# A vision tower on one Trainium2 core: LayerNorm rows on ScalarE, four score quarters in one piece, another order

## What is computed

```python
h = tok(x)                       # 3x3 depthwise convolution, then mean of 8x8 blocks: 64 tokens an image
h = h + attn0(layernorm(h))      # one head of 128
h = h + moe(layernorm(h))        # 2 shared and 8 routed experts of 512, the best 2 of 8 for each token
h = h + attn1(layernorm(h))      # 8 heads of 16; 64 keys and 15 compressed keys, a sink; rotary
h = h + mlp(layernorm(h))        # two lower-triangular 128x128 matrices along the channels, GELU

def layernorm(x):
    m, v = mean(x), var(x)       # over the 128 channels
    return (x - m) / sqrt(v + 1e-5)
```

## Time and profile before

| | us |
|---|---|
| median of 3 runs | 1969.28 |
| lowest and highest of them | 1950.70, 1969.51 |
| the profiled execution | 1981.56 |
| its span, first to last instruction | 1979.8 |

### The profile page before, as it was taken

How to read it: one execution, slowest core, us unless ns; L and a number is a source line. 1 busy time by engine, 2 the same in 40 slices (tenths; PEclk the granted TensorE clock), 3 DMA queues, 4 the chain that set the end, 5 groups by cost and what they waited for, 6 DMA issues and landing times.

```text
span 1979.8 us, 42922 instructions
## 1 busy us (share of the span) xinstructions
PE 1588.2 (80%) x14896; PEld 1190.4 (60%) x14896; DVE 1417.9 (72%) x3372; ACT 1002.2 (51%) x2581; POOL 797.3 (40%) x643
## 2 busy tenths in 40 slices
PE   0132878989898988989898989898898989998846
PEld 0021665757666675767576676667676766666623
DVE  3767677878877787888778788778887787642322
ACT  0112546555555646565555547365656555564622
POOL 2335363544526263545436263625444352504020
PEclk9975888998879797998889789879989897979965
DMA  7556564453735544554536455445546364202000
GB/s 295 216 192 230 195 221 181 162 208 145 260 134 193 211 170 163 196 202 155 211 143 227 172 188 220 143 178 201 205 141 231 140 240 156 62 7 62 13 22 6
DMA packets 109125, 331.56 MB, mean 167 GB/s; under 512 B 13662, under 2 KB 87585, under 8 KB 92412
## 3 DMA queue, kind: packets, MB, share of 16 engines
q1 hardware_dynamic: 86416, 300.90, 41.3%
q0 software_dynamic: 8992, 19.42, 2.9%
q10 hardware_dynamic: 13516, 8.50, 1.4%
HBM read 299.48 MB, written 29.29 MB: 166 GB/s over the span
## 4 chain that ended last, share of the span: by engine, by line
PE 43%; DVE 18%; POOL 15%; issue 11%; DMA 6%; ACT 5%; ACTq 2%; SPq 0%; POOLq 0%; DVEq 0%
PE hid_bank L597 10%; PE sec_bank L651 5%; POOL yg L1375 5%; POOL xbuf L1364 4%; DMA xbuf<-in_x 4%; PE hid_bank L582 3%; PE sec_bank L671 3%; PE sec_bank L662 3%; PE hid_bank L581 3%; DVE xbuf L1064 3%; DVE xbuf L1060 3%; POOL rows_d L1353 2%; DVE xc L1269 2%; POOL rs L1336 2%; PE hid_bank L583 2%
## 5 line engine op out<-in xcount | busy, mean ns | idle before, releaser
L1364 POOL TENSOR_TENSOR xbuf<-xbuf 128x512 f32<-128x512 f32 x256 | 343.3, 1341 | 587.3 <-DVE xbuf L1060 578.7
L597 PE MATMUL hid_bank<-w_s,hid 128*128 x1920 | 329.5, 324 | 0.0
L842 ACT ACTIVATE hid<-hid_bank,bias_t 128x128 f32<-128x128 f32 x960 | 272.1, 377 | 83.2 <-PE hid_bank L583 78.9
L597 PEld LDWEIGHTS hid_bank<-w_s,hid 128*128 128x128 f32 x1920 | 278.4, 223 | 18.7
L581 PE MATMUL hid_bank<-xt,w_b 128*128 128x128 bf16 x960 | 221.1, 239 | 57.8 <-ACT ys L852 30.3
L1060 DVE TENSOR_TENSOR xbuf<-xbuf 128x1536 f32<-128x1536 f32 x128 | 224.3, 1752 | 19.8 <-DMA xbuf<-in_x 19.8
L1353 POOL DMA_INDIRECT rows_d<-x2r,spot_i x128 | 159.5, 1246 | 195.8 <-DVE owned L1211 163.4
L582 PE MATMUL hid_bank<-xt,w_b 128*128 128x128 bf16 x960 | 222.2, 240 | 0.4
L583 PE MATMUL hid_bank<-xt,w_b 128*128 128x128 bf16 x960 | 218.4, 236 | 0.0
L1085 DVE SCALAR_TENSOR_TENSOR taps<-pooled_s,tapw,taps 128x256 f32<-128x256 f32 (+1 forms) x416 | 208.6, 501 | 8.3
L1068 DVE TENSOR_TENSOR xbuf<-xbuf 128x1024 bf16<-128x1024 f32 x128 | 173.5, 1355 | 24.2 <-DMA xbuf<-in_x 24.2
(11 more groups left out here) (216 smaller groups left out, 3344.2 us busy)
## 6 DMA issues: line engine op xcount, KB each, us to landing
xbuf<-in_x SPq DMA_DIRECT2D x128, 2048.0 KB
rows_s<-rows_d SPq DMA_DIRECT2D x48, 320.0 KB, 8.1
outs_d<-ys SPq DMA_DIRECT2D x240, 64.0 KB, 1.8
out<-h ACTq DMA_DIRECT2D x16, 256.0 KB
w_s<-in_w ACTq DMA_DIRECT2D x1, 2560.0 KB
hid<-in_w POOLq DMA_DIRECT2D x10, 256.0 KB, 3.4
rows_d<-x2r,spot_i POOLq DMA_INDIRECT x128
yg<-outs_d,spot_i POOLq DMA_INDIRECT x128
```

The lines of the kernel that those rows point to most:

```text
L597: mm = nc.tensor.matmul(hid_bank[n % 2][:, 0:P], hid[:, n % RING, q * P:(q + 1) * P], w_q, start=False, stop=q == FC - 1)
L842: ins = nc.scalar.activation(hid[:, n % RING, cols], hid_bank[n % 2][:, cols], ACT.Gelu, bias=bias_t[:, q, j:j + 1])
L1364: nc.gpsimd.tensor_tensor(v[:, :, 1, :], v[:, :, 1, :], v[:, :, 2 * k + 3, :], ALU.add) \
```

## The change

Three things change. First, `normalise` moves from DVE to ScalarE. DVE makes nb = -mean x inverse root, one instruction of 128x4 (`centre`), and ScalarE gives x times the inverse root plus nb (`Identity` with a scale and a bias per row), four instructions a set. There are four new ScalarE pieces, `norm1` to `norm4`, for x1, x2, x3 and x3.

Second, a `score` piece holds both halves of the heads: two masks, one to each bank, and then the four combinations of two images and two halves. There are four such pieces in place of eight on PE; DVE keeps its eight. The two halves lie in different rows of the array, the two images in different columns.

Third, the lists in `ORDER` are new for all five engines.

```diff
 ORDER = dict(
     pool="""
-        scatter.3' scatter.4' scatter.5' scatter.6' scatter.7' gather.0 gather.1 gather.2 gather.3 gather.4
+        scatter.6' gather.0 scatter.7' gather.1 gather.2 gather.3 gather.4 add.0.0 add.0.1 gather.5 gather.6
...
                 elif kind == "score":
-                    t, half = n // 2, n % 2
-                    bank = sec_bank[half]
+                    t = n
...
-                    if n >= 2:
-                        eng.wait_ge(s3_step, at(s3_step, g, 2 * (n - 2) + 2))
-                    wide, rows = bank[:, 0:HH * (LK + 1)], slice(half * C // 2, (half + 1) * C // 2)
-                    nc.tensor.matmul(wide, place_b[:], limit_b[:, half].rearrange("p h k -> p (h k)"),
-                                     start=True, stop=False)
+                    for half in range(2):
+                        if n >= 1:
+                            eng.wait_ge(s3_step, at(s3_step, g, 2 * (2 * n - 2 + half) + 2))
+                        nc.tensor.matmul(sec_bank[half][:, 0:HH * (LK + 1)], place_b[:],
+                                         limit_b[:, half].rearrange("p h k -> p (h k)"), start=True, stop=False)
                     for im in range(2):
                         tok = (2 * t + im) * L
-                        mm = nc.tensor.matmul(
-                            wide[im * L:(im + 1) * L].rearrange("p (h k) -> p h k", h=HH)[:, :, 0:LK],
-                            q3[rows, tok:tok + L], keys_h[rows, :, 2 * t + im, :],
-                            start=False, stop=True)
-                    mm.then_inc(scored, 1)
+                        for half in range(2):
+                            rows = slice(half * C // 2, (half + 1) * C // 2)
+                            wide = sec_bank[half][im * L:(im + 1) * L, 0:HH * (LK + 1)]
+                            mm = nc.tensor.matmul(wide.rearrange("p (h k) -> p h k", h=HH)[:, :, 0:LK],
+                                                  q3[rows, tok:tok + L], keys_h[rows, :, 2 * t + im, :],
+                                                  start=False, stop=True)
+                            if im == 1:
+                                mm.then_inc(scored, 1)
...
+            def normalise(g, dst, src, nb, rs, centred, ready):
+
+                eng.wait_ge(centred, at(centred, g, 1))
+                for t in range(T):
+                    nc.scalar.activation(dst[:, t, :], src[:, t, :], ACT.Identity, bias=nb[:, t:t + 1],
+                                         scale=rs[:, t:t + 1]).then_inc(ready, 1)
...
-            def normalise(g, dst, src, mv, rs, rstd, ready, read=None, need=0):
+            def centre(g, nb, mv, rs, rstd, centred):
                 eng.wait_ge(rstd, at(rstd, g, 1))
-                if read is not None and after(g, 1):
-                    eng.wait_ge(read, at(read, g - 1, need))
-                for t in range(T):
-                    nc.vector.tensor_scalar(dst[:, t, :], src[:, t, :], mv[:, t, 0:1], rs[:, t:t + 1],
-                                            ALU.subtract, ALU.mult).then_inc(ready, 1)
+                nc.vector.scalar_tensor_tensor(nb[:], mv[:, :, 0], -1.0, rs[:], ALU.mult, ALU.mult).then_inc(centred, 1)
```

92 lines of the change are left out of this document (52 added, 40 removed).

## The result

The kernel after takes 1904.11 us (median of 4 runs, 1898.11 to 1911.73), the kernel before 1969.39 (4 runs, 1950.70 to 1989.49): the ratio is 0.9668, with a 95% interval of 0.9628 to 0.9708. The forecast was 1911. Its profiled execution took 1911.73 us, with a span of 1910.0 and a mean granted clock of 0.93 (0.866 before).

The account below looks back on a forecast made before the run. PE was taken to bound the steady part; -3.8 (scores) -2.5 (head) -1.3 (xc) +0.8 +1.7 +1.2 = -3.9 us an iteration, times 15 = 58, gave 1911 us. Range 1845 to 1978, likeliest case 1885 to 1940.

Parts of the forecast that it names:

- quarters, PE's work: Score pieces on PE: four array quarters run side by side, four pieces replace eight; 3.8 us less an iteration.
- DVE empties the banks: Between score pieces: PE waits for DVE to empty both banks, mostly covered by other work; 0.8 us more an iteration.
- split ahead of score.0, exponentials ahead of att.7: Before the first score piece and att.7: PE waits for ScalarE's key split and exponentials; 1.7 us more an iteration.
- xc: Compressed keys on PE: xc comes before DVE's second rotation, so PE's wait for it goes; 1.3 us less an iteration.
- first lift waits for h: Iteration's first lift on PE: POOL's adds come sooner, the wait for h falls from 2.1 to 0.8 us.
- `out'` waits for taps: Transposes of `out'`, two down pieces later on PE: wait for the last tap goes, 1.2 us less; bound 0.
- LayerNorm longer through ScalarE: norm3 and norm4, on the chain to PE: each set 0.6 us longer through ScalarE, 1.2 us more an iteration.
- The rival of no change: Score stage stays as long as DVE's emptying makes it; only the head gains: 1968, or up to 1950; chance 18%.
- Head: Start of the iteration: PE's waits for h and for the last taps shrink, together 2.5 us less an iteration.
- Keys: Compressed keys and score start: PE's wait for xc goes (-1.3 us), waits for ScalarE's split and exponentials come (+1.7).
- The rival (17%): Clock no longer falls at the scores once PE's xc wait goes: 3.6 us more gain an iteration, 1864 us; 17%.
- The slower rival: SP's queue at the iteration turn: x and rows.0 land late, +3.6 us an iteration, 2023 us; chance 18%.

Follow-up runs that it names:

- e9: Changed kernel with only the new order left: score halves one after the other, LayerNorm on DVE; 1959.89 us, 0.9607 of the kernel before, second chip.
- e4: Changed kernel with the LayerNorm rows back on DVE, so new order and quarters; 1943.64 us, 0.9540 of the kernel before, second chip.
- e1: Changed kernel with the two score halves of a piece one after the other, LayerNorm on ScalarE kept; 1966.29 us, 0.9669 of the kernel before, second chip.
- e3: Kernel before with only the LayerNorm rows moved to ScalarE; 1995.81 us, 1.0144 of the kernel before.
- e10: Changed kernel with `out'` later as in e6 and the LayerNorm rows back on DVE; 1916.32 us, 0.9732 of the kernel before.
- e6: Changed kernel with `out'` two pieces later on PE and one on ScalarE; 1896.83 us, 0.9615 of the kernel before.
- e12: Changed kernel with POOL's list of the kernel before; 1917.67 us, 0.9749 of the kernel before.
- e13: Changed kernel with DVE's second rotation and first inner work put back ahead of xc; 2000.53 us, 1.0157 of the kernel before.
- e5: Kernel before with six extra matmuls on PE in place of its wait for xc; 1967.56 us, 0.9935 of the kernel before.

## Why the prediction was right, step by step

The total was right: 1911 against 1904.11, inside the likeliest case's own range. Its terms were not, and errors of some us each cancel, so that the total came this close is luck. It gave 3.9 us an iteration where the traces have 5.7 (65 us by the medians, over 15 iterations, is 4.4). Each term per iteration:

| step | forecast | measured |
|---|---|---|
| quarters, PE's work | -3.8 | -3.1 (by the pieces), -3.3 (e9 to e4), -4.3 (e1 to after, two chips) |
| the same in time | -3.8 | -1.1 (e9 to e4) |
| DVE empties the banks | +0.8 | 0.4 (4.4 / 12) |
| split ahead of score.0, exponentials ahead of att.7 | +1.7 | 1.3 ((5.4 + 5.2 + 4.6) / 12) |
| xc | -1.3 | -1.3 (15.9 / 12, gone) |
| first lift waits for h | -1.3 | -0.9 (22.4 to 11.1 in 12) |
| `out'` waits for taps | -1.2 | +0.9 (18.8 to 29.3 in 12) |
| LayerNorm longer through ScalarE | +1.2 | +0.4 (e9 to e1), +1.8 (e3), -1.3 (e10 to e6) |
| clock | 0 | PE's work -4.4 (before to e9, two chips), time -2.6 (long stretches, within before) |
| waits behind the scores | 0 | +2.2 (26.6 / 12) |

The rows don't form one sum, since part of the new waits is what the quarters' saved work turned into. In PE's own account the work falls by 8.6, some 3.1 of it by the quarters and the rest with the clock, and the waiting grows by 2.9.

**Scores.** The numbers on PE were near: four quarters in 0.76 us, 1.07 a piece without a wait (1.17 forecast), 3.1 us less work. (Its own figures, 8.3 and 4.7, give 3.6; it took 3.8. The 1.04 that it started from had a small lift in it, and a piece alone took 0.92.) The step that failed is that the work taken away from PE was put down as time, since "PE, not DVE, is the bound". PE was the bound of the iteration, not of this stage: in the new order DVE's list takes 13.8 us there with or without quarters. The rival of no change had named this mechanism with 18%; it holds for the score term, 2.7 us of the 3.8, though not for the kernel.

**Head.** The forecast counted two waits of PE and took both away. The first fell as said (0.9 left, 0.8 forecast). The second had 0 as its bound, with the words that a late tap list moves along; it did more than that. One more tap stands behind the turn of the iteration on DVE now, ends.0.0 (1.28 us) stands ahead of the last tap where it stood behind it, and the two adds, brought forward as forecast, run beside DVE's taps and stretch them by 2.1 us (e12 undoes that). Both waits are ends of one chain on DVE, and e6 and e12 shift the wait from one to the other. A step that names only who waits, and not what DVE has to do in that stretch, can't see this.

**Keys.** Right, both in the wait that went and in the one that came at score.0. But e13 shows that this step can't be priced by the row of before: there PE waits 1.3 us behind seven pieces of other work between `att.4` and the compressed keys, and the new list has spent the filler elsewhere. Undone in the new order the step costs 91 us, not 20.

**Clock.** The rival (17%) gave 3.6 us an iteration from the two levels of the earlier trace rows and named the wait for xc as the cause. The size was about right: the low stretch of the score stage is gone in every iteration, and PE works 4.4 us less from before to e9. (By the kernel before alone it is 2.6 us of time an iteration. The prediction set one of the two shortest of the twelve iterations against the mean, and it put PE's busy time at 95 to 98, where one iteration has 101.3.) The cause isn't borne out: e5 fills the wait and keeps the long low stretch; e13 has a wait four times as long and no long stretch in the scores. The stretch goes with the order of the lists; which of their moves does it was not isolated. In the sum it stood at 0. So more of the gain came by the clock than by the scores.

**LayerNorm.** ScalarE's work rose from 61.7 to 67.0 us, 5.3 (6.2 forecast), DVE's fell by 3.7 and not 5.2. Rows of the kernel after, from a grouping by line and shape over the twelve iterations (busy us, mean ns), and two of the kernel before for the same lines over eleven (L1068 is now L1085, L1364 now L1381):

```profile
L1381 POOL TENSOR_TENSOR xbuf<-xbuf 128x512 f32<-128x512 f32 x192 | 302.9, 1578 | 271.5 <-DVE xbuf L1077 265.1
L1077 DVE TENSOR_TENSOR xbuf<-xbuf 128x1536 f32<-128x1536 f32 x96 | 168.1, 1751 | 13.5 <-DMA xbuf<-in_x 13.1
L1085 DVE TENSOR_TENSOR xbuf<-xbuf 128x1024 bf16<-128x1024 f32 x96 | 155.8, 1623 | 0.0
...
L785 ACT ACTIVATE x<-h,nb,rs 128x128 f32<-128x128 f32 x144 | 59.5, 499 | 4.6 <-DVE nb L1070 4.5
```
```profile
L1364 POOL TENSOR_TENSOR xbuf<-xbuf 128x512 f32<-128x512 f32 x176 | 231.5, 1315 | 367.7 <-DVE xbuf L1060 362.0
...
L1068 DVE TENSOR_TENSOR xbuf<-xbuf 128x1024 bf16<-128x1024 f32 x88 | 119.8, 1362 | 2.9 <-DMA xbuf<-in_x 2.8
```

The activation with two pointers takes 499 ns, 480 forecast. That DVE lost less than counted is the row of L1085: it takes 261 ns longer each, 8 x 0.26 = 2.1 us an iteration, of which L1081 gives back 1.0 (745 ns against 866).

**The slower rival** is not at work: DVE waits for x 13.1 / 12 = 1.1 us an iteration (L1077), under the 2 named. As announced, PE waits for the split, and for xc no more. PE's wait for L1216's successor is under 1 us on average, and PE's busy time has fallen by more than the 3 us that were named as the sign for the scores, but over half of these 8.6 by the clock, so that this sign says less than it was meant to.

## What to carry to other kernels

Ask of each stage whose list takes longest there before work saved on the engine that bounds the iteration is counted as time: here 3.3 us of TensorE's work saved went with 1.1 of time. Price a wait by everything that the waited-for engine has in that stretch, since a piece moved past one wait only meets the next, and look at what a third engine will do beside it (POOL's earlier adds cost DVE's taps 2.1 us); and a piece's filler is part of its price, so a step is worth what it is in the new list (91 us here) and not in the old one (20). And look where the granted clock is low before and after in each variant: the one part that changed no instruction, the order, brought as much as the whole change, and with it the long low stretches of the score stage were gone.
